# Attention over heads by scores first, a new division between the engines, and deviations by Exp and Ln

## What is computed

```
fq = elu(q) + 1;  fk = elu(k) + 1
kv    = einsum('bhnd,bhne->bnde', fk, v)        # sum over heads
qkv   = einsum('bhnd,bnde->bhne', fq, kv)
qk    = einsum('bhnd,bnd->bhn', fq, fk.sum(axis=1))
attn  = qkv / (qk[..., None] + 1e-06)
...
x = q_x + attn @ wo + bo
h = _ln(x, ln2_w, ln2_b)
x = x + gelu(h @ fc_w + fc_b) @ proj_w + proj_b
```

## Time and profile before

| | |
|---|---|
| time, median of 3 runs | 1933.11 us (1931.91 to 1933.52) |
| the profiled execution | 1932.89 us, its span 1931.2 us |
| busy share of the span | PE 91%, DVE 73%, POOL 65%, PE's weight loads 60%, ACT 42% |
| mean granted PE clock | 0.93 of full |

### The profile page before, as it was taken

One profiled execution on the slowest core, in us unless ns is written; L12 is line 12 of the kernel. 1 busy time (PEld: TensorE's weight loads), 2 busy tenths in 40 slices (PEclk: granted clock), 3 DMA queues, 4 the chain that ended last, 5 costly groups with the idle time before them and its releaser, 6 DMA issues.

```text
span 1931.2 us, 28717 instructions
## 1 busy us (share of the span) xinstructions
PE 1751.4 (91%) x6826; PEld 1154.0 (60%) x6886; DVE 1400.1 (73%) x2645; ACT 812.8 (42%) x1526; POOL 1260.7 (65%) x742
## 2 busy tenths in 40 slices
PE   3489998898898988988989889897999999999997
PEld 1255565555555655655566556555777777776775
DVE  8888898988988989889889899614444444444443
ACT  3145455464554563654544645431333323332332
POOL 5876888988988888789888888803333333333333
PEclk8688898898998988989989889889999999999999
DMA  4112110110101101101011010103333433433333
GB/s 161 64 57 109 44 44 22 44 37 28 44 11 44 44 22 44 41 24 44 11 44 44 22 44 34 41 6 87 61 58 60 60 60 60 60 60 57 59 60 49
DMA packets 75753, 94.90 MB, mean 49 GB/s; under 512 B 8400, under 2 KB 69712, under 8 KB 74448
## 3 DMA queue, kind: packets, MB, share of 16 engines
q0 software_dynamic: 25584, 34.75, 11.2%
q1 hardware_dynamic: 50144, 59.85, 9.8%
HBM read 49.18 MB, written 45.38 MB: 49 GB/s over the span
## 4 chain that ended last, share of the span: by engine, by line
PE 83%; ACT 5%; POOL 5%; DVE 3%; issue 2%; DMA 1%; POOLq 0%; ACTq 0%; DVEq 0%
PE p_b L1189 18%; PE p_b L1237 11%; PE p_b L1268 10%; PE p_q L1325 9%; PE p_b L1325 9%; PE p_b L1341 9%; PE p_q L1161 5%; PE p_b L1260 3%; PE p_v L1161 3%; PE p_v L1333 2%; PE p_b L1175 2%; POOL prod_pool L445 2%; PE p_xT L1315 1%; DMA out_rows<-prod_pool,prod 1%; ACT bT L612 1%
## 5 line engine op out<-in xcount | busy, mean ns | idle before, releaser
L557 POOL DMA_INDIRECT out_rows<-prod_pool,prod x135 | 209.7, 1553 | 402.8 <-DMA out_rows<-prod_pool,prod 376.9
L445 POOL TENSOR_TENSOR prod_pool<-prod_pool 128x544 f32<-128x544 f32 (+4 forms) x240 | 399.7, 1665 | 18.8
L1237 PE MATMUL p_b<-bT,fc_sb 128*128 128x512 f32 x512 | 226.6, 601 | 12.1 <-ACT bT L655 12.1
L1189 PE MATMUL p_b<-proj_sb,hid 128*128 128x256 f32 x1024 | 230.5, 379 | 0.0
L812 DVE TENSOR_REDUCE kvT<-prod 128x128 f32<-128x2048 f32 x96 | 219.4, 2286 | 2.7
L804 DVE TENSOR_TENSOR prod<-p_q,v_dve 128x4096 f32<-128x4096 f32 x48 | 211.8, 4413 | 0.0
L1268 PE MATMUL p_b<-bT,sgup_sb 128*128 128x512 f32 x384 | 208.2, 700 | 0.0
L1189 PEld LDWEIGHTS p_b<-proj_sb,hid 128*128 128x128 f32 x1024 | 189.7, 190 | 27.7 <-issue 0.5
L1341 PE MATMUL p_b<-exp_sb,prod 128*128 x810 | 197.5, 380 | 0.8 <-DVE prod L1123 0.8
L1123 DVE COPY prod<-p_v 128x384 f32<-128x384 f32 x135 | 75.2, 557 | 164.4 <-PE p_v L1333 164.4
L1325 PE MATMUL p_q<-exp_sb,prod 128*128 x544 | 186.9, 487 | 0.7 <-ACT prod L710 0.7
(11 more groups left out here) (165 smaller groups left out, 2831.5 us busy)
## 6 DMA issues: line engine op xcount, KB each, us to landing
prod<-rows_sorted SPq DMA_DIRECT2D x135, 130.0 KB, 3.3
exp_sb<-in_experts SPq DMA_DIRECT2D x8, 1152.0 KB, 10.3
xin<-in_x SPq DMA_DIRECT2D x16, 512.0 KB, 3.5
xres<-in_x SPq DMA_DIRECT2D x16, 512.0 KB, 3.4
out_rows<-x SPq DMA_DIRECT2D x16, 512.0 KB, 3.0
out_rows<-prod_pool,prod POOLq DMA_INDIRECT x135, 4.0
rows_sorted<-rows,slot POOLq DMA_INDIRECT x128, 2.6
rows_sorted<-pad_row SPq DMA_DIRECT2D x1, 1040.0 KB, 5.7
```

The lines of the kernel that those rows point to most:

```text
L445: done(g.tensor_tensor(prod_pool[:, at:at + n * w], prod_pool[:, at:at + n * w], prod_pool[:, at + n * w:at + 2 * n * w], ALU.add))
L557: pool.indirect_dma_start(out=out[:, :], out_offset=bass.IndirectOffsetOnAxis(ap=tok_i[j], axis=0), in_=yg[j], in_offset=None, compute_op= ...
L1189: ins = t_.matmul(o, src[:, k, t * P:(t + 1) * P], w[:, k, :], start=k == 0, stop=bias_at is None and k == chunks - 1)
L1237: ins = t_.matmul(bnk[:], fc_sb[:, k, f * P:(f + 1) * P], bT[:, k, :], start=k == 0, stop=k == KC - 1)
```

## The change

Attention over heads is computed by scores. A DVE tile is now: `features`; `products_1` (16 x 16 x 16 = 4096 products of q and k), `sums_1` (in one or two pieces, written to PSUM), `totals` (the denominators, a sum over 16), `products_2` (4096 products of scores and v), `sums_2`, then `guard`, `inverse` and `divide`. DVE does tiles 1 and 3 with all 16 heads and tile 2 (SPLIT) with 8 heads. POOL does its own tile and the other 8 heads (POOL_HEADS) of tile 2, both in the same two steps, `scores` and `mixed`, each with four halvings. The order of POOL's round is new, and `pool_v_used` is announced by `mixed` of its own tile, the last products of the round. k is projected head by head (in `b_tok` and `wqkv`, `inner` is gone from k), v as before. The residual after the MLP and its statistics are done in two halves with `sums_1` of tile 3 between them. The standard deviations' reciprocals come from ACT alone, as Exp(-0.5 Ln(var)), in a table set that holds Exp and Ln (`table_exp_ln`, an explicit load), in place of Sqrt with a table load and DVE's reciprocal. The diff, cut to its core:

```diff
-DVE_HEADS = 12
-POOL_HEADS = HEADS - DVE_HEADS
+SPLIT = 2
+POOL_HEADS = 8
...
+            def scores(q, k, n):
+                return g.tensor_tensor(
+                    prod_pool[:, 0:n * HH].rearrange("p (d h g) -> p d h g", d=HD, g=HEADS),
+                    q.rearrange("p (h d) -> p d h", d=HD).unsqueeze(3).to_broadcast([P, HD, n, HEADS]),
+                    k.rearrange("p (g d) -> p d g", d=HD).unsqueeze(2).to_broadcast([P, HD, n, HEADS]), ALU.mult)
+            def mixed(sc, v, n):
+                return g.tensor_tensor(
+                    prod_pool[:, 0:n * HH].rearrange("p (g h e) -> p g h e", g=HEADS, e=HD),
+                    sc.rearrange("p h g -> p g h").unsqueeze(3).to_broadcast([P, HEADS, n, HD]),
+                    v.unsqueeze(2).to_broadcast([P, HEADS, n, HD]), ALU.mult)
+            def heads(c):
+                wait(pool, feat_ready, 4 * c + SPLIT + 1)
+                announce(pool, scores(features[:, (HEADS - POOL_HEADS) * HD:D], features[:, D:2 * D], POOL_HEADS),
+                         share_qk_used, c + 1)
+                announce(pool, halve(flat(s_pool[:, own, :])), pool_s, c + 1)
+                announce(pool, mixed(s_pool[:, own, :], v_dve[SPLIT % 2][:].rearrange("p e g -> p g e"),
+                                     POOL_HEADS), share_v_used, c + 1)
+                done(halve(flat(qkv_pool[:, own, :])))
...
             def body(c, core, stage_b, tail):        # POOL
+                if core:
+                    wait(pool, feat_ready, 4 * c + 1)
+                    announce(pool, scores(fqk_pool[:, 0:D], fqk_pool[:, D:2 * D], HEADS), pool_qk_used, c + 1)
                 if tail and (core or stage_b):
                     gate_shared(c)
                 if core:
-                    wait(pool, feat_ready, 4 * c + 1)
...
-                    heads(c, 1)
-                    announce(pool, halve(kv_pool[:].rearrange("p d e -> p (d e)"), first=4), pool_v_used, c + 1)
+                    wait(pool, attn_ready, c)
+                    done(halve(flat(s_pool[:, 0:HEADS, :])))
                 if tail:
                     scatter(c)
...
                 if core:
-                    heads(c, 2)
...
-                    heads(c, 3)
+                    heads(c)
+                    announce(pool, mixed(s_pool[:, 0:HEADS, :], v_pool[:], HEADS), pool_v_used, c + 1)
+                    announce(pool, halve(flat(qkv_pool[:, 0:HEADS, :])), pool_qkv, c + 1)
...
+            def rsqrt(out, var, log, std, n):        # ACT
+                a.activation(var, var, ACT.Ln).then_inc(log, 1)
+                act.wait_ge(log, n)
+                a.activation(out, var, ACT.Exp, scale=-0.5).then_inc(std, 1)
...
+                table_exp_ln()
                 if core:
                     take_qkv(c, 3)
...
                 if stage_b:
-                    table(ACT.Sqrt)
                     wait(act, x1_read, c)
-                    a.activation(sq_b[:], sq_b[:], ACT.Sqrt).then_inc(ln3_std, 1)
+                    rsqrt(rs_b[:, 0, :], sq_b[:], ln3_log, ln3_std, c)
...
             def scales_b(std, scale, c):             # DVE
                 wait(dve, std, c)
-                done(v.reciprocal(rs_b[:, 0], sq_b[:]))
...
                 if core:                             # DVE's body
-                    divide_and_sum(c, 2)
-                    q_products(c, 2, True)
-                    q_sums(2)
+                    n = own_heads(2)
+                    sums_1(2, 0, n)
+                    totals(2, den_0[:, 0:n])
+                    products_2(c, 2, False)
+                    guard(den_0[:, 0:n])
+                    sums_2(2)
+                    inverse(den_0[:, 0:n])
                     features(c, 3)
-                    kv_products(3)
-                if stage_b:
-                    residual_2(c)
+                    done.sync()
+                    done.later(divide(1, 0, qkv[0][:, 0:n], den_0[:, 0:n]))
+                    release(c, 2)
+                    products_1(3)
+                if stage_b:
+                    residual_2(c, 0)
+                if core:
+                    sums_1(3, 0, HEADS)
+                if stage_b:
+                    residual_2(c, 1)
                     scales_b(ln3_std, ln3_scale, c)
```

More of the change, by code:

```diff
@@ L771, in ln1_scales @@
                 wait(dve, ln1_std, b + 1)
-                done(v.reciprocal(rs_a[:, 0:2], sq_a[:]))
                 v.scalar_tensor_tensor(rs_a[:, 2:4], mv_a[:, :, 0].unsqueeze(1).to_broadcast([P, 2, TPB]), -1.0,
@@ new lines, in features, with own_heads @@
+                if u == 0:
+                    feature(fqk_pool, 0, 2 * D).then_inc(feat_ready, 1)
+                else:
+                    own = own_heads(u) * HD
+                    done.later(feature(e, D, 2 * D))
+                    if own < D:
+                        done.later(feature(e, own, D))
+                    feature(y, 0, own).then_inc(feat_ready, 1)
+                    dve.wait_ge(feat_ready, n + 1)
+            def own_heads(u):
+                return HEADS - POOL_HEADS if u == SPLIT else HEADS
@@ L818, in kv_sums_1, with sums_1, totals @@
+            def sums_1(u, lo, hi):
                 done.sync()
-                done.later(kv_sum(u, 0))
-            def kv_sums_2(c, u):
+                done.later(v.tensor_reduce(
+                    p_qk[u % 2][:, lo * HEADS:hi * HEADS],
+                    prod[:, lo * HH:hi * HH].rearrange("p (a d) -> p a d", d=HD), AX.X, ALU.add))
+            def totals(u, at):
                 done.sync()
-                announce(dve, kv_sum(u, 1), share_ready, 3 * c + u)
-            def q_products(c, u, free):
+                n = own_heads(u)
+                done.later(v.tensor_reduce(at, p_qk[u % 2][:, 0:n * HEADS].rearrange("p (h g) -> p h g", h=n),
+                                           AX.X, ALU.add))
@@ L971, in body @@
                         ln1_stats(c + 1)
-                    kv_sums_2(c, 1)
-                    q_products(c, 1, last)
+                    sums_1(1, half, HEADS)
+                    totals(1, den_1[:, 0:HEADS])
+                    products_2(c, 1, False)
                     if not last:
                         ln1_scales(c + 1)
+                    guard(den_1[:, 0:HEADS])
+                    sums_2(1)
+                    inverse(den_1[:, 0:HEADS])
+                    if not last:
                         dve.wait_ge(ln1_scale, c + 2)
-                        dve.sem_inc(pq_free, 1)
-                    q_sums(1)
+                    wait(dve, attnT_psum, KC * c)
                     features(c, 2)
-                    kv_products(2)
+                    done.sync()
+                    done.later(divide(0, 0, qkv[1][:], den_1[:, 0:HEADS]))
+                    release(c, 1)
+                    products_1(2)
                 if tail:
@@ L999, in body @@
                         stand_alone(dve)
+                    totals(3, den_0[:, 0:HEADS])
+                    if stage_b:
+                        dve.wait_ge(ln3_scale, c)
+                    products_2(c, 3, True)
+                    wait(dve, pool_s, c + 1)
+                    done.later(v.tensor_reduce(den_0[:, HEADS:2 * HEADS + POOL_HEADS], s_pool[:], AX.X, ALU.add))
                 if stage_b:
```

210 lines of the change are left out of this document (91 added, 119 removed).

## The result

The changed kernel takes 2045.97 us (median of 4 runs, 2044.89 to 2046.3) against 1932.63 for the kernel before in the same runs: 1.0586 times as long, interval 1.0571 to 1.0601. The direction was forecast; the size was not, 113 us where 39 were forecast, and the time lies outside the range. The profiled span is 2044.6 us, 113.4 more than before.

What follows compares the result with a forecast made beforehand. A loop through POOL's `mixed`, ACT's v copy and PE was taken to bound: 2.0 + 23.4 + 54.5 = 79.9 us a block. With head and tail, +38.8 us: 1932.9 + 38.8 = 1971.7, about 1972; range 1940 to 1998.

Steps and rivals of the forecast that it cites:

- The loop: ACT's v copy waits for POOL's last `mixed`, PE for ACT, `gate_shared` for PE: 79.9 us a block, 3.1 more.
- T to R: From the end of POOL's own-tile `mixed` (T) to PE resuming after ACT's first third-norm `norm` (R): 2.0 us.
- POOL's part: From the start of POOL's `gate_shared` to the end of its own-tile `mixed`: 54.5 us.
- rivals 1, 2 and 3: POOL's products: cheaper, about 1919 us (chance 0.10); step costs nothing, 1947 (0.13); strided at one and a half times, 1994 (0.07).
- PE's leg: From PE resuming after the third norm's first `norm` (R) to the start of POOL's `gate_shared`: 23.4 us, kept unchanged.
- What would show it: Trace signs: PE idle about 7 us before R, R to `gate_shared` 23 to 24, R to R near 80.
- rival 4: DVE's features of tile 2 reach POOL's `heads` about 2 us late: 81.9 us a block, 1997 us, chance 0.10.
- The head: Start up to the first R (R1): 144.2 us against 143.45 before, since block 0's attention waits for POOL.
- The tail: After the last R, PE no longer waits for POOL's late last attention: 1.7 us come back.
- The table load: Gone before the third norm: 0.45 us a block even without the loop; at the second norm taken as nothing.
- The halves of the residual: `residual_2` split around `sums_1`: DVE's statistics end near R + 74.2, before T at R + 77.9, so no gain.

Runs made afterwards that it cites:

- the first experiment: Changed kernel with the expert numbers copied to `rows` from `first2` in PSUM instead of `top_i` in SBUF (the mended cast): 1962.54 us, ratio 1.0153.
- both repairs: Changed kernel with the expert numbers copied from PSUM and ACT's copy to `v_pool` moved behind the third norm: 1902.41 us, ratio 0.9846.

## Why the prediction was right, and where it was wrong

- **The loop.** Right. The copy of v waits for `mixed`, the third norm behind it, PE behind that. Moving that copy is worth 60 us on top of the mended cast (1962.5 to 1902.4).
- **T to R.** 2.0 forecast, 1.71 measured.
- **POOL's part.** 54.5 forecast, 54.52 measured (684.69 to 739.21). The rates by step were right: in the groups of the changed kernel 4096 products take 9.480 us read across and 7.533 read contiguously, 9.5 and 7.6 forecast. The three products between `gate_shared` and T take 17.3 us, as forecast (4.875, 4.886, 7.533), so rivals 1, 2 and 3 are out. An element read across costs 26% more (2.27 against 1.79 ns). The Trainium skill (GPSIMD Engine Reference, "Performance pitfalls for Q7 kernels") gives about 50% for reads with a step over 8 bytes; the measurement decides.
- **PE's leg.** This is the step that failed. 23.4 was carried over from the kernel before and measured as 29.1, in all blocks: 3.6 us of waiting for `chosen` and 1.7 of low clock behind it. The forecast's sentence, "With a longer pause before R the clock is low at R as it is now, so I leave it there", looked at PE's own work and its clock alone and didn't ask what DVE hands to PE there, and what POOL would be doing by then. It could have been worked out from the kernel before. There DVE comes to the copy at R + 10.65 (692.26), beside a short sum of POOL, and PE uses `chosen` at R + 13.5. In the new order `scores` run from about T + 9.3, R + 7.3, to R + 16.8: the copy would end there, `chosen` near R + 17.4, and PE would wait about 3.9 us; 3.6 were measured. 5.7 us in thirteen blocks are 74.1 of the missing 74.6; the rest (T to R −3.8, the head −0.4, the tail +4.6) nearly cancels.
- **What would show it.** R to `gate_shared` of 23 to 24 was given as a mark, and it is this one that fell. PE's idle time before R, about 7 us forecast, is 6.6; DVE's wait for Exp is 5.5 us, 4 forecast; POOL waits 11.7 before `gate_shared` instead of 5 to 7, since PE's leg is longer (5.9 in the mean without the hold), and for no other engine before `heads`, as said, so rival 4 is out.
- **The head.** R1 forecast at 144.2, measured 143.85.
- **The tail.** −1.7 forecast. In the first experiment, without the hold, the rest behind the fourteenth R is 784.3 us against 788.8, −4.5; in the changed kernel +2.9.
- **The forecast without the hold.** 1972 against 1962.5 in the first experiment: 0.4 us a block too long (79.9 against 79.5), 1.8 at the head (R1 at 142.4, forecast 144.2) and 2.8 in the tail.
- **The table load.** Called almost worthless; alone in the kernel before it is worth 10 us, with the repairs 26. The step that failed is the one on the second norm, "PE is then in the down projection; taken as nothing". It asked what PE was doing, not what stands behind the wait on DVE. In the kernel before DVE's waits there are a row of their own, 1.5 us a block:

```profile
DVE rs_b L779 <- ACT sq_b L645: 23.5, 16, 1.9
```

  With Exp and Ln this wait is 0.4. How much of it the loop leaves in the changed kernel was not tried.
- **The halves of the residual.** "Splitting buys nothing here" fits: with both repairs, undoing it gives 3 us. In the changed kernel itself it was not tried.

The fastest kernel, 1899.22 us, has the change's attention and its Exp and Ln, with v copied behind the norm, the numbers copied from PSUM and the residual in one. It is 33 us faster than before. Its parts are not additive: without Exp and Ln the kernel with both repairs is 4 us faster than before, Exp and Ln alone are 10, the two together 31.

## What to carry to other kernels

When an order is changed, list for every engine not only the work that moves but what the others will be running beside it: here the price of one 4-element copy went from 0.38 to 9.2 us because another engine's instruction beside it got long. A release that moves to the end of an engine's round should be followed through whatever is queued behind its waiter, and the waiter moved behind the work that others wait for. Small copies on DVE that another engine waits for are better read from or written to PSUM if POOL runs long instructions. And a wait of an engine that is not the bound is free only if nothing behind it in that engine's list is late for the bound.

## What the runs showed of the hardware

DVE instructions of three kinds, with all of their tensors in SBUF, were held until POOL's running `tensor_tensor` ended: the copy with a cast 9.20 us (4.55 with POOL's instruction in two), `tensor_scalar` 3.31, the sum of two inputs 8.97, each for 4 elements a partition. Beside the same POOL instruction a copy from PSUM took 0.17, a cast or an addition to PSUM 0.17, a comparison with one input in PSUM 0.21, and a `tensor_reduce` from SBUF to SBUF 0.22. The Trainium skill (SBUF — State Buffer, "Who interferes with whom") has the rule: DVE's second pair of SBUF ports is shared with POOL; copies, casts and `tensor_scalar` in DVE's two-port modes want it, and so does a `tensor_tensor` of two SBUF inputs beside a POOL instruction that reads SBUF; `tensor_reduce` on trn2 does not; and "Whoever issues first gets the shared pair for the whole instruction". The traces agree for the cast, `tensor_scalar`, the sum of two inputs and `tensor_reduce`, and beside POOL's `tensor_tensor` with "the whole instruction". The forecast had not weighed this rule; from it and the rows of before the new wait of PE follows.

Beside another POOL instruction the hold was shorter. In the experts' loop of the changed kernel POOL's indirect DMA instructions (L560) take 1.55 us. A DVE copy of 4 elements from SBUF to SBUF (L1139) that starts 0.53 us behind the start of one takes 0.50 us and ends 1.03 us behind it; one that starts 0.2 to 0.5 us or 0.86 to 1.2 us behind it takes 0.17.

The clock took back part of what was gained and added to what was lost: behind a wait of 3.6 us the projection took 3.63 us instead of 1.96, and with a pause shorter by 0.8 us before R the low level ended 1.5 us later, with the same block.
